# The first mixing of a conditioned residual chain on four 32-row tiles, from the fourth example on

## The reference

```python
def mix(x, embedding, ...):                 # layers 0 and 2
    att = softmax(mlp(embedding))
    agg_w = einsum('bk,koi->boi', att, weight[..., 0])
    return einsum('boi,bih->boh', agg_w, x) + (att @ bias_k)[:, :, None]

def conv(x, c, weight, c_weight, bias):     # layers 1 and 3
    out = conv_general_dilated(x, weight, (1,), [(4, 4)], feature_group_count=4)
    return out + einsum('nd,od->no', c, c_weight)[:, :, None] + bias[None, :, None]

x = x + mix(x, ...); x = x + conv(x, ...); x = x + mix(x, ...); x = x + conv(x, ...)
```

## Time and profile before

| what | value |
| --- | --- |
| median of three runs | 2654.9 us |
| the profiled execution, its own time | 2653.38 us |
| its span, first to last instruction | 2651.6 us |
| TensorE busy with matmuls | 99% of the span |
| VectorE, ScalarE, GpSimd busy | 81%, 77%, 31% |
| 16 DMA engines, mean busy share | 58.3% |
| data moved by DMA | 489.82 MB |
| TensorE's granted clock, share of full | 0.998 |

### The profile page before, as it was taken

One profiled execution on the slowest core, in us unless ns is written; L12 is line 12 of the kernel. 1 busy time (PEld: TensorE's weight loads), 2 busy tenths in 40 slices (PEclk: granted clock), 3 DMA queues, 4 the chain that ended last, 5 costly groups with the idle time before them and its releaser, 6 DMA issues.

```text
span 2651.6 us, 107002 instructions
## 1 busy us (share of the span) xinstructions
PE 2629.5 (99%) x42614; PEld 1811.0 (68%) x42614; DVE 2147.0 (81%) x3095; ACT 2039.0 (77%) x3613; POOL 825.5 (31%) x1040
## 2 busy tenths in 40 slices
PE   8999999999999999999999999999999999999997
PEld 6667666766676667666766676667666766676665
DVE  8988788878887888788878887888788878887883
ACT  7777777777777777777777777777777777777775
POOL 1233323232323332333333332333233323332332
PEclk9999999999999999999999999999999999999999
DMA  4565556555655565556555655565556555655554
GB/s 163 182 199 191 180 181 194 191 180 181 193 191 180 182 194 190 180 183 194 189 180 183 195 189 180 183 196 187 180 184 197 186 180 184 197 185 180 185 182 138
DMA packets 228046, 489.82 MB, mean 185 GB/s; under 512 B 47016, under 2 KB 129072, under 8 KB 195376
## 3 DMA queue, kind: packets, MB, share of 16 engines
q1 hardware_dynamic: 228016, 489.39, 58.3%
HBM read 205.04 MB, written 150.99 MB: 134 GB/s over the span
## 4 chain that ended last, share of the span: by engine, by line
PE 98%; DVE 1%; SPq 0%; ACT 0%; issue 0%; DMA 0%; DVEq 0%
PE ps L361 42%; PE ps L342 28%; PE ps L313 14%; PE ps L326 13%; SPq L214 0%; DVE xp L643 0%; DVE y L667 0%; DVE y L673 0%; DVE m_sum L625 0%; PE ps L264 0%; PE ps L259 0%; DVE prod L622 0%; DMA o_ch<-o_ph 0%; ACT y_full L486 0%; PE ps L301 0%
## 5 line engine op out<-in xcount | busy, mean ns | idle before, releaser
L361 PE MATMUL ps<-y,conv_parts 32*128 32x512 f32 x18432 | 1143.3, 395 | 2.9 <-DVE y L673 1.1
L361 PEld LDWEIGHTS ps<-y,conv_parts 32*128 32x128 f32 x18432 | 907.3, 183 | 282.9 <-issue 129.1
L766 POOL COPY bias<-bias_table 128x4 f32 (+3 forms) x512 | 323.8, 633 | 1788.4 <-DMA o_ch<-o_ph 895.1
L673 DVE TENSOR_TENSOR y<-y_full,y 128x512 fp32r<-128x512 f32 x1020 | 636.5, 687 | 232.6 <-ACT y L492 232.6
L342 PE MATMUL ps<-y_full,conv_raw 32*32 32x512 f32 (+1 forms) x16384 | 753.8, 596 | 2.6 <-ACT y_full L486 2.6
L486 ACT ACTIVATE y_full<-ps,bias 128x512 f32<-128x512 f32 x1020 | 605.0, 707 | 26.5 <-issue 16.1
L541 ACT ACTIVATE o_ph<-ps,bias 128x512 f32<-128x512 f32 x510 | 309.8, 693 | 378.1 <-PE ps L361 371.4
L492 ACT CAST y<-y_full 128x512 fp32r<-128x512 f32 x1020 | 566.8, 663 | 0.0
L342 PEld LDWEIGHTS ps<-y_full,conv_raw 32*32 32x32 f32 (+1 forms) x16384 | 275.0, 116 | 409.8 <-issue 406.6
L772 POOL COPY o_t<-o_ch 128x512 f32<-128x512 f32 x508 | 528.7, 1189 | 30.0 <-DMA o_ch<-o_ph 30.0
L486 ACT ACTIVATE y<-ps,bias 128x512 fp32r<-128x512 f32 x516 | 313.2, 690 | 190.8 <-PE ps L342 176.4
(11 more groups left out here) (56 smaller groups left out, 67.0 us busy)
## 6 DMA issues: line engine op xcount, KB each, us to landing
x_t<-x SPq DMA_DIRECT2D x128, 1024.0 KB, 5.0
o_ch<-o_ph SPq DMA_DIRECT2D x2032, 64.0 KB, 2.0
out<-o_t SPq DMA_DIRECT2D x127, 1024.0 KB, 4.0
m_parts<-mixed SPq DMA_DIRECT2D x512, 128.0 KB, 2.6
mixed<-m_own SPq DMA_DIRECT2D x128, 128.0 KB, 1.7
conv_raw<-conv_w SPq DMA_DIRECT2D x2, 768.0 KB, 10.5
mix_sb<-mix_w SPq DMA_DIRECT2D x2, 576.0 KB, 7.7
out<-x_t SPq DMA_DIRECT2D x4, 256.0 KB, 4.2
```

Source lines behind the costliest of these rows:

```text
L361: ins = nc.tensor.matmul(ps[:, bank + t, :], conv_parts[layer][rows, w, s - DENSE[0], :], src[rows, a, p_in, q:q + N], start=first, stop=f ...
L673: nc.vector.tensor_tensor(dst, full, high.bitcast(fp32), ALU.subtract).then_inc(low_set[layer], 1)
L766: nc.gpsimd.tensor_copy(bias[layer][:], bias_table[:, bass.ds(j, 1), COLUMN[layer]:COLUMN[layer] + WIDTH[layer]].rearrange("c j g -> c (j ...
```

## The change

From the fourth example on (`WHOLE = 3` keep the old form) the first mix has the form of the second. x is loaded by quarters of time: lanes 32q to 32q + 31 hold the 32 channels of each of four groups g for quarter q. The first mix' matrix halves are stored to HBM and loaded into four places like the second's, into a tile of their own, and 48 matmuls on 32 rows take the place of 12 on 128 rows. All four banks are begun in the first group of four matmuls and finished in the last. On SyncE the store stands first in a step, the loads behind those of x. The wait for the second matrix' store moves from its loads into the last group of shuffles.

```diff
+    WHOLE = 3
-        m_parts = sb("m_parts", [128, G, 2, C], f32r)
+        m_parts = {l: sb(f"m_parts{l}", [128, G, 2, C], f32r) for l in MIXES}
...
             def load_x(j):
-                sp.dma_start(flat(x_t, "q n"), x[j]).then_inc(x_in, 16)
+                if isinstance(j, int) and j < WHOLE:
+                    sp.dma_start(flat(x_t, "q n"), x[j]).then_inc(x_in, 64)
+                    return
+                for q in range(G):
+                    sp.dma_start(x_t[CG * q:CG * (q + 1)],
+                                 x[j].rearrange("(g c) (q n) -> q c g n", g=G, q=G)[q]).then_inc(x_in, 16)
...
+            def load_matrix(layer, j, first):
+                if layer == 0:
+                    sp.wait_ge(mm[0], 4 * j)
+                    sp.wait_ge(stored[0], 16 * j - 16 * (WHOLE - 1))
+                elif not first:
                     sp.wait_ge(mm[2], 4 * j)
-                sp.wait_ge(stored, 16 * j + 16)
                 for q in range(G):
+                    sp.dma_start(m_parts[layer][CG * q:CG * (q + 1)].rearrange("c g w o -> c g (w o)").bitcast(fp32),
+                                 scratch[layer // 2][bass.ds(j, 1)].rearrange("s (g c) w o -> (s c) g (w o)", g=G)).then_inc(m_in[layer], 16)
...
+            def shuffle(j, g, matrix):
                 sp.wait_ge(phases_set, nth(j, g))
                 for p in range(PH):
+                    if p == 1 and matrix is not None:
+                        sp.wait_ge(stored[2], 16 * matrix + 16)
                     sp.dma_start(o_ch[CG * g:CG * (g + 1), p, :], o_ph[CG * p:CG * (p + 1), g, :]).then_inc(shuffled[p], 16)
...
             def step(i, inner, odd):
+                tiled = has(i, inner, -2) and (inner or i + 2 >= WHOLE)
+                if tiled:
+                    store_matrix(0, i + 2)
                 if has(i, inner, -3):
                     sp.wait_ge(x_low_set, 4 * (i + 3))
                     load_x(i + 3)
+                if tiled:
+                    load_matrix(0, i + 2, False)
                 if has(i, inner, 2):
                     sp.wait_ge(in_time_set, 4 * (i - 1))
                     sp.dma_start(out[i - 2], o_t[:]).then_inc(out_done, 16)
                 if has(i, inner, -1):
-                    store_matrix(i + 1)
+                    store_matrix(2, i + 1)
...
+            def first_mix(j, wait_bank):
+                pe.wait_ge(m_in[0], 16 * G * (j - WHOLE + 1))
+                for g in range(G):
+                    pe.wait_ge(x_low_set, nth(j, g))
+                    for n, (m, a) in enumerate(PASSES):
+                        first, final = g == 0 and n == 0, g == G - 1 and n == len(PASSES) - 1
+                        for q in range(G):
+                            rows = slice(CG * q, CG * (q + 1))
+                            if first:
+                                wait_bank(q)
+                            ins = nc.tensor.matmul(ps[:, q, :], m_parts[0][rows, g, m, :], xp[rows, a, g, :], start=first, stop=final)
+                            if final:
+                                ins.then_inc(mm[0], 1)
...
             def halves(layer, j, first=False):
                 dve.wait_ge(summed[layer], j + 1)
-                if not first and layer == 0:
-                    dve.wait_ge(mm[0], 4 * j)
+                if layer == 0 and isinstance(j, int) and j <= WHOLE:
+                    if not first:
+                        dve.wait_ge(mm[0], 4 * j)
+                elif layer == 0:
+                    dve.wait_ge(stored[0], 16 * j - 16 * WHOLE)
                 elif not first:
-                    dve.wait_ge(stored, 16 * j)
+                    dve.wait_ge(stored[2], 16 * j)
...
-    scratch = nc.dram_tensor("mixed", (B, C, 2, C), mybir.dt.float32, kind="Internal").ap()
+    scratch = nc.dram_tensor("mixed", (2, B, C, 2, C), mybir.dt.float32, kind="Internal").ap()
```

More of the change, by code:

```diff
@@ L123, in build_cond_resid @@
         own_set = {l: sem(f"own_set{l}") for l in MIXES}
-        stored = sem("stored")
+        stored = {l: sem(f"stored{l}") for l in MIXES}
         x_high_set, x_low_set = sem("x_high_set"), sem("x_low_set")
@@ L131, in build_cond_resid @@
         x_in = sem("x_in")
-        m_in = sem("m_in")
+        m_in = {l: sem(f"m_in{l}") for l in MIXES}
         shuffled = [sem(f"shuffled{p}") for p in range(PH)]
@@ L191, in load_x, with store_matrix @@
             def load_x(j):
[L193 to L203 removed]
+                if isinstance(j, int) and j < WHOLE:
[4 more added lines that the diff above has]
+                                 x[j].rearrange("(g c) (q n) -> q c g n", g=G, q=G)[q]).then_inc(x_in, 16)
+            def store_matrix(layer, j):
+                sp.wait_ge(own_set[layer], j + 1)
+                sp.dma_start(scratch[layer // 2][bass.ds(j, 1)].rearrange("s c w o -> (s c) (w o)"),
+                             flat(m_own[layer], "w o").bitcast(fp32)).then_inc(stored[layer], 16)
+            def load_matrix(layer, j, first):
[3 more added lines that the diff above has]
+                elif not first:
                     sp.wait_ge(mm[2], 4 * j)
[L205 removed]
                 for q in range(G):
[L207 to L210 removed]
+                    sp.dma_start(m_parts[layer][CG * q:CG * (q + 1)].rearrange("c g w o -> c g (w o)").bitcast(fp32),
+                                 scratch[layer // 2][bass.ds(j, 1)].rearrange("s (g c) w o -> (s c) g (w o)", g=G)).then_inc(m_in[layer], 16)
+            def shuffle(j, g, matrix):
                 sp.wait_ge(phases_set, nth(j, g))
                 for p in range(PH):
+                    if p == 1 and matrix is not None:
+                        sp.wait_ge(stored[2], 16 * matrix + 16)
                     sp.dma_start(o_ch[CG * g:CG * (g + 1), p, :], o_ph[CG * p:CG * (p + 1), g, :]).then_inc(shuffled[p], 16)
@@ L233, in step @@
                 if has(i, inner, -1):
-                    store_matrix(i + 1)
-                if has(i, inner, 1) and (inner or not is_last(i)):
+                    store_matrix(2, i + 1)
+                moves = has(i, inner, 1) and (inner or not is_last(i))
+                if moves:
                     for g in range(G):
-                        shuffle(i - 1, g)
+                        shuffle(i - 1, g, i + 1 if g == G - 1 and has(i, inner, -1) else None)
                 if has(i, inner, -1):
-                    load_matrix(i + 1, False)
+                    if not moves:
+                        sp.wait_ge(stored[2], 16 * (i + 2))
+                    load_matrix(2, i + 1, False)
                 if not inner and is_last(i):
@@ L246, in _ @@
             load_x(1)
-            store_matrix(0)
-            load_matrix(0, True)
+            store_matrix(2, 0)
+            sp.wait_ge(stored[2], 16)
+            load_matrix(2, 0, True)
             sp.wait_ge(x_low_set, 8)
@@ L325, in second_mix @@
                             rows = slice(CG * p, CG * (p + 1))
-                            ins = nc.tensor.matmul(ps[:, 4 + p, :], m_parts[rows, g, m, :], y2[rows, a, g, :], start=first, stop=final)
+                            ins = nc.tensor.matmul(ps[:, 4 + p, :], m_parts[2][rows, g, m, :], y2[rows, a, g, :], start=first, stop=final)
                             if final:
@@ L409, in step @@
                     second_mix(i)
-                if has(i, inner, -2):
+                if not inner and i + 2 < WHOLE:
+                    first_mix_whole(i + 2, free0)
+                elif has(i, inner, -2):
                     first_mix(i + 2, free0)
```

10 lines of the change are left out of this document (5 added, 5 removed).

## The result

The changed kernel takes 3370.5 us (median of 6 runs) against 2654.5 us for the kernel before: ratio 1.270, interval [1.269, 1.272]. The forecast of 2633 us is wrong in size and in sign. What it called "The matrix comes late" has happened, at ten times the highest price that it was given. The rest of this part reads the profiled execution (3366.0 us).

The account below looks back on a forecast made before the run. TensorE's matmuls, covering 99% of the span, were taken as the bound. From 2653.4 us, 24 kept (125 x 0.19) came off and 2 for the start went on: 2631.4, against the median 2633; range 2603 to 2655.

Parts of the forecast that it names:

- The matrix comes late: Rival: first mix' matrix loads late on SyncE by L, mean step grows L / 2; 2660 to 2726 us, chance 0.15.
- Landing: First mix' last matrix load lands 2.6 to 3.9 us after issue, margin 1.1 to 2.4 us; costed at nothing.
- TensorE: First mix' 12 matmuls become 48, in 12 groups at 0.233 us: no change by itself.
- the front end: Start of the first mix: its 0.23 us gain is eaten whole by the wait for the fourth bank's eviction.
- Both ends gained: Rival: at the first mix' start the fourth bank's wait costs nothing; 50 us less, 2607 us, chance 0.16.
- Weight loads not hidden: Rival: mix groups wait for weights, 0.34 us instead of 0.233, 1.3 us more a step; 2792 us, chance 0.03.
- SyncE's queue: Eight more DMAs a step on SyncE take 3.6 us; output store slips to 1320.0, shuffles keep their place.
- ScalarE and VectorE: Evictions after the first mix start some 0.6 us later; 0.6 us of ScalarE's wait stays, nothing on the path.
- Start: Fourth example's mix up to 1.5 us late, next one or two likewise: 2 us in all, bounds 0 and 5.

Follow-up runs that it names:

- experiment 6: The changed kernel with x loaded by one 1 MB load instead of four quarters, so the mix computes on x in the wrong lanes: 2673.6 us.
- Experiment 4: The changed kernel with GpSimd's copies of the output into time order cut to 16 of each 512 columns: 2756.5 us.
- experiment 5: The changed kernel with 16 extra matmuls in front of each first mix' wait, overwritten by the mix: 3123.5 us.
- experiment 3: The changed kernel with only the first matrix' store moved ahead of the last group of shuffles, its loads still behind x's: 3240.2 us.
- version 2: The changed kernel with the first matrix' loads ahead of x's wait and loads, and its store in the previous step's shuffles: 2637.0 us, ratio 0.994.
- experiment 9: version 2 with ScalarE's fourth eviction of the output cut to 64 of 512 columns in the changed steps: 2624.0 us, ratio 0.9895.
- experiments 7 and 8: The kernel before with x in four loads, by lanes (32 lanes x 8 KB) or by times (128 lanes x 2 KB): 2654.9 and 2655.4 us.
- experiment 1: The changed kernel with SyncE's four loads of the first matrix put ahead of x's wait and loads: 2805.3 us, ratio 1.056.

## Why the prediction was wrong

**The step that failed is *Landing*:** "The last matrix load lands 2.6 us (median) to 3.9 us (longest) after issue", "The margin is 1.1 to 2.4 us", "I cost it at nothing, and the cover is that margin." The landing took 6.3 us, so the working is off by 2.4 to 3.7. Everything ahead of it was about right: from the start of the first mix to the end of x's low halves I had 1315.81 - 1304.82 = 10.99 us, and the quiet loop has 2.68 + 8.27 = 10.95; from there to the last load begun I had 1319.6 - 1315.81 = 3.8, and it took 1339.85 - 1336.49 = 3.4. With 2.6 to 3.9 for the landing the loop closes in 17.4 to 18.7 us, inside TensorE's 20.19. With the 6.3 measured and 0.3 from there to the start of the mix it takes about 21, outside. I had taken the landing from matrix loads with nothing queued ahead of them; here they stand behind 1 MB in four loads for 32 lanes each; behind the same 1 MB in one load it was 4.2 to 4.6 (experiment 6). I had named the queueing ("there the quarters of x, the new 512 KB and the output store will queue") and not priced it.

**The rival's price failed too.** "The matrix comes late" had a loop of two steps, with "the mean step grows by L / 2 because the next shuffles start from a dense stage that was not delayed", and at most L = 1.5. I had followed the queue through the shuffles and taken the time of x's low halves as given. But these come behind the first mix on ScalarE and VectorE, and SyncE holds the matrix loads behind the loads of x that wait for them: a loop of one step, in which nothing halves a delay. The bare loop's 21.2 us is 1.1 longer than the 20.12 that TensorE takes when nothing waits. That is within the 1.5 that I had, but it is paid whole: 0.8 us a step over the kernel before, where the rival's highest price, at half, was 0.57 (20.95 against 20.38). Experiment 4 lost 102 us by it.

**What no step had** is the other 614 us (3370.5 - 2756.5). Once TensorE idles in front of the mix, the granted clock in it falls to 0.62 (shown: experiment 5 holds the clock, and the mix goes back from 4.23 us to 2.68, first group to last). GpSimd's copies come to run beside VectorE's subtractions, which then take about twice as long (shown: experiment 4). Both lie inside the loop, so what they add is paid in every step. The shift of the stages against each other is what brings copies and subtractions together: the trace of experiment 3 shows it, where a mix 0.6 us later against the shuffles is enough. In the changed kernel they meet from its first changed step on, where TensorE already waits 4.43 us; that its start puts it there is read from the timeline alone.

**What was right.** *TensorE*: with the loop cut (version 2) the step takes 20.12 us, forecast 20.19, and the kernel 2637.0, forecast 2633. That the two times lie within 4 us is in part luck: the step gained 0.26 us where I had 0.19, and the slow first steps took back more than the 2 us that I had put. In its timeline the fourth eviction ends at 1336.40, the fourth weight load starts at 1336.45, 0.05 us behind, and the second group of that tile at 1336.80: the front end as it was worked out. "Both ends gained" is out, as the wait for the fourth bank is real. *Weight loads not hidden* is out: 48 matmuls take 2.80 us in experiment 9, and the pace of the earlier trace rows holds. *SyncE's queue*: x's four loads take 1.83 us and the matrix' four 1.74, where I had 1.8 each, and one store 0.37. What I had not counted is that a queue in order passes on its waits: its cost in instructions was right, and x's wait in front of the matrix loads was the harm. *ScalarE and VectorE* at about nothing holds only while the copies don't coincide with them. The term *Start* had the fourth example's mix up to 1.5 us late. In the changed kernel it waits 4.43 us, the loop's first turn; in version 2 it begins at 61.34, no later than before, and the five steps behind it give up the 6 us.

## What to carry to other kernels

When loads are put behind others in one engine's queue, write down the whole loop, from the reader back through the wait at the head of the queue to the same reader one step before, and compare its sum with the bound engine's step; a load that is "free" in issue time can still close such a loop. Price its landing behind what stands ahead of it, at the rate that those transfers get into their lanes, and not from loads that found the queue empty. A tuned pipeline that misses by a little may lose far more than the miss, so a margin of a microsecond needs a bound on what happens beyond it; here moving the matrix' loads and its store in the order, without a byte less, turned 27% slower into 0.6% faster.

## What the runs showed of the hardware

- The same 1 MB in four loads landed at 228 GB/s (median) into 32 lanes at a time, in pieces of 8 KB, and at 305 over all 128 lanes, in pieces of 2 KB (experiments 7 and 8).
- A subtraction 128 x 512 with two SBUF operands took 684 ns alone and 1452 (median) while GpSimd copied in SBUF (experiment 3); GpSimd's copy took 1561 ns in the mean in the changed kernel and 1189 in the one before.
- Four row tiles of 32 x 128, in twelve groups of 512 columns, finished in 2.80 us, the pace of twelve 128-row matmuls (0.232 us each); between two such stages in a row nothing was lost when the banks were free (the chain of experiment 9).
- SyncE took 0.37 us for a store, 0.44 to 0.46 for a load in a row of four, and 0.63 to 0.76 for a shuffle, in the mean of sixteen; with 31 DMAs a step its queue, with one wait of 1.5 us in it, bounded the kernel of experiment 1 at 21.5 us.
